# ScalarE takes the normalizing and the division of the router's weights in a fused four-layer kernel's last layer

## The reference

```python
x = x + _L3_xattn_ref(_layernorm(x, axis=-1), ctx_2048, itok_BxS_0_1023, ...)
x = x + _L3_ffn_ref(_layernorm(x, axis=-1), L3_ffn_gate_w, ...)

def _layernorm(x, axis=-1, eps=1e-05):
    m = jnp.mean(x, axis=axis, keepdims=True)
    v = jnp.var(x, axis=axis, keepdims=True)
    return (x - m) / jnp.sqrt(v + eps)

def _L3_ffn_ref(hidden_states, gate_w, gate_proj_w, up_proj_w, down_proj_w):
    x = hidden_states.reshape(-1, h)
    router_logits = x @ gate_w
    routing_weights, selected = jax.lax.top_k(router_logits, K)
    routing_weights = jax.nn.softmax(routing_weights, axis=-1)
    ...
    gate = jax.lax.ragged_dot(hidden_sorted, gate_proj_w, group_sizes)
    up = jax.lax.ragged_dot(hidden_sorted, up_proj_w, group_sizes)
    down = jax.lax.ragged_dot(jax.nn.silu(gate) * up, down_proj_w, group_sizes)
    ...
    out = jnp.sum(out * routing_weights[..., None], axis=1)
```

## Time and profile before

| | us |
|---|---|
| median of 3 runs | 755.91 |
| lowest and highest run | 755.21, 762.36 |
| profiled execution, its own time | 756.39 |
| its span on the core | 754.7 |
| mean granted TensorE clock | 0.953 of full |
| TensorE busy | 662.2 (88% of the span) |
| VectorE busy | 600.8 (80%) |
| ScalarE busy | 480.1 (64%) |
| GpSimd busy | 417.5 (55%) |

### The profile page before, as it was taken

The page is one execution under the profiler, slowest core; times in us unless marked ns, Lnnn a source line. Parts: engine busy times, 40 slices in busy tenths (PEclk is TensorE's granted clock), DMA queues, the critical chain, the costliest instruction groups (busy, mean ns, idle before and its releaser), DMA issues.

```text
span 754.7 us, 14577 instructions
## 1 busy us (share of the span) xinstructions
PE 662.2 (88%) x5052; PEld 552.6 (73%) x5052; DVE 600.8 (80%) x1657; ACT 480.1 (64%) x1203; POOL 417.5 (55%) x535
## 2 busy tenths in 40 slices
PE   2998969885799989969998988988888999999974
PEld 1887857663479845748887877877667999999942
DVE  6567368988956878888788998998788899999666
ACT  3543557956845378747776666666434699999810
POOL 2444683994610226414555377578774277777764
PEclk9999996989989999999999999999999899999998
DMA  8987003400010050039100011014336399999393
GB/s 326 311 263 249 8 2 83 145 1 1 3 44 1 1 210 2 1 110 369 41 1 1 1 48 56 33 49 175 106 134 218 116 318 320 314 322 314 121 374 141
DMA packets 47522, 100.63 MB, mean 133 GB/s; under 512 B 7349, under 2 KB 27782, under 8 KB 45940
## 3 DMA queue, kind: packets, MB, share of 16 engines
q1 hardware_dynamic: 40196, 82.46, 32.2%
q0 software_dynamic: 7248, 17.18, 6.2%
HBM read 60.17 MB, written 43.12 MB: 137 GB/s over the span
## 4 chain that ended last, share of the span: by engine, by line
PE 40%; DVE 34%; ACT 12%; POOL 6%; issue 5%; DMA 3%; SPq 0%; DVEq 0%; POOLq 0%; ACTq 0%
PE bank L320 9%; PE bank L321 8%; PE bank L322 8%; DVE sc L2036 3%; DVE qf L2050 3%; PE bank L2637 3%; DVE qf L2045 2%; ACT p L1988 2%; DVE X L2452 2%; DVE st L346 2%; ACT p L973 2%; DVE HN L366 1%; POOL hl L781 1%; DVE op6l L2025 1%; DVE qs L2044 1%
## 5 line engine op out<-in xcount | busy, mean ns | idle before, releaser
L2848 POOL DMA_INDIRECT rows_out<-ye,di x87 | 95.8, 1101 | 42.6 <-ACT ye L2725 21.5
L2085 POOL TENSOR_SCALAR p<-p,ri 128x256 f32<-128x256 f32 x128 | 74.0, 589 | 75.9 <-DVE ri L2030 75.1
L1988 ACT ACTIVATE p<-sc,mn 128x256 f32<-128x256 f32 x128 | 64.1, 502 | 37.3 <-DVE mn L2036 37.2
L2315 POOL DMA_INDIRECT slots_in<-row,si x64 | 67.2, 1050 | 16.6 <-issue 15.3
L320 PE MATMUL bank<-x7h,w7h 128*96 128x192 f32 x232 | 63.7, 275 | 0.0
L321 PE MATMUL bank<-x7l,w7h 128*96 128x192 f32 x232 | 59.4, 256 | 0.0
L322 PE MATMUL bank<-x7h,w7l 128*96 128x192 f32 x232 | 59.2, 255 | 0.0
L360 POOL TENSOR_TENSOR rs<-ve,neghalf 128x2 f32<-128x2 f32 x32 | 23.2, 728 | 58.4 <-DVE ve L354 58.0
L320 PE MATMUL bank<-w7h,h7h 96*128 96x256 f32 x164 | 49.2, 300 | 5.8 <-DVE h7l L2428 4.9
L1925 PE MATMUL bank<-ident,p 128*128 128x128 f32 x256 | 41.1, 284 | 14.1 <-POOL p L2085 13.5
L2142 DVE TENSOR_TENSOR w7l<-w7f,w7h 128x640 fp32r<-128x640 f32 x60 | 48.9, 815 | 2.4 <-ACT w7h L2137 2.1
(11 more groups left out here) (448 smaller groups left out, 2579.0 us busy)
## 6 DMA issues: line engine op xcount, KB each, us to landing
w7f<-in_w SPq DMA_DIRECT2D x64, 320.0 KB, 4.4
xe<-slots_in SPq DMA_DIRECT2D x29, 432.0 KB, 5.3
slots_in<-zt SPq DMA_DIRECT2D x7, 1728.0 KB, 19.1
rows_out<-zt SPq DMA_DIRECT2D x8, 1024.0 KB, 10.2
rw<-rows_out SPq DMA_DIRECT2D x4, 2048.0 KB, 9.5
w0raw<-in_w SPq DMA_DIRECT2D x3, 768.0 KB, 10.8
wo<-in_w_o SPq DMA_DIRECT2D x1, 2048.0 KB
raw<-in_w SPq DMA_DIRECT2D x2, 704.0 KB, 4.9
```

Of the source, the lines that this page charges most:

```text
L1988: a = A.activation(m.p6[k2 % 5][:, s, :], m.sc6[k2 % 3][:, s, :], ACT.Exp, bias=m.mn6[k2 % 5][:, s:s + 1], scale=-1.0, accum_out=m.su6[k2 ...
L2085: i = G.tensor_scalar(m.p6[j][:, s, :], m.p6[j][:, s, :], m.ri6[j][:, s:s + 1], 1.0, ALU.mult, ALU.mult)
L2315: G.indirect_dma_start(out=m.buf_in, out_offset=bass.IndirectOffsetOnAxis(ap=m.si7[:, t, j:j + 1], axis=0), in_=m.row7[:, t, :], in_offset ...
L2848: G.indirect_dma_start(out=m.buf_out, out_offset=bass.IndirectOffsetOnAxis(ap=m.di7[:, q:q + 1], axis=0), in_=m.ye7[q % NY][:], in_offset= ...
```

## The change

For pairs 0 to 2 in the attention stage the normalizing goes from VectorE to ScalarE. ScalarE computes it as `x * rs + sh`, so GpSimd makes the shift `sh = -mean * rs` first (`gpsimd_shift`, two instructions of one column, one for each tile, at ago 1 right behind the power). Pair 3's normalizing in `head` stays on VectorE. For all four pairs the division of all experts' weights by their sum (two instructions of 128x64) goes from VectorE to ScalarE, at ago 15 in `l3x` and after `h7h` of i = 3 in `head`; VectorE keeps the product of exponentials and mask.

```diff
-    def gpsimd_apply(self, g):
-
+    def gpsimd_shift(self, g):
         G, m = self.nc.gpsimd, self.m
         for t in (2 * g, 2 * g + 1):
             G.wait_ge(*self.rstd.at(g + 1))
             G.tensor_scalar(m.sh[:, t:t + 1], m.mv[:, t, 0:1], m.rs[:, t:t + 1], -1.0, ALU.mult,
                             ALU.mult).then_inc(self.shift.sem, 1)
+
+    def scalar_apply(self, g):
+        A, m = self.nc.scalar, self.m
+        for t in (2 * g, 2 * g + 1):
+            A.wait_ge(*self.shift.at(t + 1))
+            A.activation(self.rows[:, t, :], m.X[:, t, :], ACT.Identity, bias=m.sh[:, t:t + 1],
+                         scale=m.rs[:, t:t + 1]).then_inc(self.hn.sem, 1)
...
@@ l3x, scalar()
                 g, ago = routing(k)
+                if ago == 2:
+                    r.norm.scalar_apply(g)
...
+                if ago == 15:
+                    r.scalar_weights(g)
@@ l3x, vector()
-                if ago == 2:
-                    r.norm.vector_apply(g)
@@ l3x, gpsimd()
                 if ago == 1:
                     r.norm.gpsimd_rstd(g)
+                    r.norm.gpsimd_shift(g)
@@ Router
         V.tensor_tensor(m.wt7[:, p, :], m.ex7[:, 2 * (g % 2):2 * (g % 2) + 2, :],
                         m.mk7[:, 128 * g:128 * g + 128].rearrange("p (m n) -> p m n", m=2),
-                        ALU.mult).then_inc(self.wt.sem, 1)
-        V.wait_ge(*self.wt.at(3 * g + 1))
-        V.wait_ge(*self.rw.at(12 * g + 11))
+                        ALU.mult).then_inc(self.chosen.sem, 1)
+
+    def scalar_weights(self, g):
+        A, m = self.nc.scalar, self.m
+        A.wait_ge(*self.chosen.at(g + 1))
+        A.wait_ge(*self.rw.at(12 * g + 11))
         for t in (2 * g, 2 * g + 1):
-            V.tensor_scalar(m.wt7[:, t, :], m.wt7[:, t, :], m.r7[:, t:t + 1], None, ALU.mult).then_inc(self.wt.sem, 1)
+            A.activation(m.wt7[:, t, :], m.wt7[:, t, :], ACT.Copy, scale=m.r7[:, t:t + 1]).then_inc(self.wt.sem, 1)
@@ head, scalar()
             dense.scalar_high(i, i)
+            if i == 3:
+                r.scalar_weights(3)
@@ head, vector()
             if i == FIRST + 1:
-                V.wait_ge(*r.wt.at(12))
+                V.wait_ge(*r.wt.at(8))
```

More of the change, by code:

```diff
@@ L375, in gpsimd_apply @@
                             ALU.mult).then_inc(self.shift.sem, 1)
+    def scalar_apply(self, g):
[4 more added lines that the diff above has]
+                         scale=m.rs[:, t:t + 1]).then_inc(self.hn.sem, 1)
+    def gpsimd_apply(self, g):
+        G, m = self.nc.gpsimd, self.m
+        self.gpsimd_shift(g)
         for t in (2 * g, 2 * g + 1):
@@ L1849, in l3x @@
     done = m.xfinal = lambda t: x.at(t + 1)
-    m.next_norm = Norm(nc, m, sig, rows=m.row7[:, :, 0:D])
+    m.next_norm = Norm(nc, m, sig, rows=m.row7[:, :, 0:D], shifted=6)
     r, w7 = m.router, m.weights = Router(nc, io, m, sig), Weights(nc, io, m, sig)
@@ L2166, in __init__ @@
         m.scattered = sig("scattered", 16 * 64)
-        self.ng, self.ex, self.wt = sig("neg_top", 4), sig("exps_router", 8), sig("router_weights", 12)
+        self.ng, self.ex, self.wt = sig("neg_top", 4), sig("exps_router", 8), sig("router_weights", 8)
+        self.chosen = sig("exps_chosen", 4)
         self.rw = sig("row_weights", 48)
```

## The result

The changed kernel takes 761.15 us (759.17 to 766.98), the kernel before 757.12 (755.21 to 762.36), 12 runs of each on the same chip: ratio 1.0067, 95% interval [1.0045, 1.0089]. It is slower, by 4.0 us between the medians (by the interval 3.4 to 6.7), and outside the predicted range. Repeated on two more occasions it gave 1.005 [1.0023, 1.0077] and 1.007 [1.0035, 1.0104]. The profiled execution took 759.63 us (span 757.9), 3.2 us more than before.

What follows compares the result with a forecast made beforehand. It took the chain of hand-overs (GpSimd ahead of TensorE, VectorE from the logits on), not VectorE's busy share, as the bound; +0.81 + 0.14 - 0.42 = +0.53 us on 755.91 gave 756.4, 8-in-10 range 752.0 to 760.0.

Steps and rivals of the forecast that it cites:

- Part 1: Normalizing leaves VectorE, pairs 0 to 2: it starts at most 0.3 us earlier, then waits for TensorE's scores; gain 0.
- the 91% share: VectorE's busy share, 120.4 of 133 us in the 400 to 533 us window; argued for winning its time in full.
- Part 2: The two `sh` join GpSimd's queue ahead of scatter and `p` scalings: +0.81 us, all in front of TensorE.
- 0.13 + 0.34 + 0.34: Net GpSimd delay at pairs 0, 1, 2: 0.60 us for `sh` less 0.47, 0.26 and 0.26 coming back.
- the upper bound: If the `sh` fall beside `Ql` and are stretched by 0.47, they cost 1.4 us more: 2.2 us.
- the reason given for the scatter: At pairs 1 and 2 VectorE's normalizing, once gone, no longer stretches GpSimd's scatter: 1.31 back to 1.05 us, 0.26 each.
- all of it: The whole +0.81 us of GpSimd's delay over pairs 0 to 2 falls in front of TensorE.
- the pause of TensorE costs its clock once more: Rival: longer pause brings pair 2 the low clock, 1.43 us more, 757.8; chance 0.18 shared with a late ScalarE.
- a late ScalarE: Rival: slow normalizing or late shift delays `pt` and exponentials, three times up to 1.0 us, 759.4; shared chance 0.18.
- Part 4: Weights' scaling moves to ScalarE: +0.07 us each at pairs 0 and 1, 0 at pair 2, -0.42 at pair 3.
- VectorE loses 0.42 us on its chain ... So `Qh` comes 0.42 earlier: Weights, pairs 0 and 1: `Qh` 0.42 us earlier, what follows 0.49 later on ScalarE, +0.07 per pair.
- Part 3: ScalarE's two normalizing instructions between `op6h` and next `pt`: about 1.0 us, nine tenths covered by idle; cost 0.

Runs made afterwards that it cites:

- e4: Changed kernel with GpSimd's shift one step later, behind the next `p` scalings, and ScalarE's normalizing one step later: 804.03 us, ratio 1.0025 to the kernel before.
- e13: Changed kernel with 16 (pair 0) and 24 (pairs 1, 2) extra TensorE products in the pause ahead of the `p` transposes: 757.59 us, ratio 0.9999.
- e14: Kernel before with 12 and 16 extra TensorE products in the pause ahead of the `p` transposes: 756.01 us, ratio 0.9979.
- e3: Kernel before with the six shift instructions added on GpSimd behind the power, read by nobody; normalizing stays on VectorE: 804.24 us, ratio 1.0048.
- e2: Kernel before with only the weights' scaling moved to ScalarE, for all four pairs: 805.89 us, ratio 1.0049.
- e5: Kernel before with the weights' scaling on ScalarE, placed ahead of `Qh` in the same step: 758.54 us, ratio 1.002.
- e1: Changed kernel with the weights scaled on VectorE again, so only the normalizing half: 802.97 us, ratio 0.999.
- e6: Kernel before with GpSimd's power one step later, behind the `p` scalings, and VectorE's normalizing one step later: 757.34 us, ratio 1.0008.
- e9: Changed kernel with power and `sh` behind `p`, ScalarE's normalizing a step later and the weights, both ahead of `Qh`: 801.9 us, ratio 1.0024; again 753.67, 0.9954.
- e7: Changed kernel with power and `sh` one step later, behind the `p` scalings, and ScalarE's normalizing one step later, behind `Qh`: 757.07 us, ratio 0.9993.
- e10: As e9, but ScalarE normalizes right behind that step's `pt`, ahead of the exponentials: 801.7 us, ratio 1.0055.
- e11: Kernel before with power behind `p`, weights on ScalarE ahead of `Qh`, VectorE normalizing between the minima and `qs`: 808.53 us, ratio 1.0088.

## Why the prediction was wrong

The forecast was +0.5 us, to 756.4, with a range of 752.0 to 760.0. Measured were 761.15 against 757.12, and for the profiled executions 759.63 against 756.39.

**Part 1, VectorE gains nothing: right.** It waits 0.81 us for `op6h` where it normalized, and longer for the scores. The chain of waits beat the 91% share.

**Part 2, +0.81 us in front of TensorE: too small, and its agreement with the outcome is luck.** The first `p` transpose starts 0.43, 0.67 and 0.66 us later behind the variance than before (2.83, 4.19 and 4.18 against 2.39, 3.52 and 3.52), together 1.76, more than twice the 0.13 + 0.34 + 0.34. The term that was mis-sized is `sh`: it costs the queue 0.9 us a pair and not 0.6, because it was stretched, which I had put at the upper bound (0.80 us for the pair where I wrote 0.50). What comes back from `p` and the scatter was about as forecast (0.47 and 0.21), though the reason given for the scatter was wrong (e4). At the logits only half of the delay is left. With the clock held full in both kernels (e13 against e14) the three stretches cost -0.05, +0.49 and +0.45, together +0.89. At pair 0 a later wait of TensorE takes it up; the changed kernel's clock held (e13) and the kernel before's (e14):

```profile
413.42 0.36 PE L1908 MATMUL bank<-qch,QW6h 96*128 96x256 f32 x1 [0.62 <-ACT hT L2229]
```

```profile
414.19 0.36 PE L1897 MATMUL bank<-qch,QW6h 96*128 96x256 f32 x1 [1.12 <-ACT hT L2214]
```

So 0.89 is close to 0.81 because two errors cancel, the second being that "all of it" would reach the end of the stretch.

The stretch beside `Ql` is what the Trainium skill, "GPSIMD Engine Reference", section Specifications, describes as contention on the shared SBUF interfaces with VectorE instructions of two SBUF inputs. The trace agrees (0.80 us beside `Ql`, 0.49 and 0.50 without), and for instructions of one column as well, which I had excused for their size.

**The step that failed: the sum carries TensorE's clock at nothing.** It appears only as a rival, "the pause of TensorE costs its clock once more", at a chance of 0.18 shared with a late ScalarE and a price of 1.43 us, once. It is what happened, and larger. The sum of the low clock rose from 6.8 to 17.0 us over the three stretches. By after minus e13 it costs 4.85 us, by before minus e14 1.13: +3.7 us from this alone. By the medians the filled pauses give back 4.5 us in the changed kernel and 1.7 in the one before, 2.8 more, with 2 to 3 us of uncertainty on each. What makes a low stretch last 6.8 us and not 3.4 behind the longer pauses is open (e3 has the pauses without it); that the clock is what costs the time, and that filled pauses take it away, is shown. I had the mechanism and the pair where it would strike, but four things wrong. The pauses grew by 1.1 us, not by 0.3: besides the 0.66 of the queue there are 0.47 us by which the variance falls further behind TensorE once the weights stand on ScalarE's chain (e2). The low stretch could also double in length (pair 1: 3.4 to 6.8). I made it wait for a pause of "about 2.6", with 2.3 not enough, though in the kernel before the clock had fallen behind pauses of 1.85 and 2.32. And I took pair 2's full clock in the one trace as a coin that could fall either way, with the gains set against the losses, where the repeats show nearly the same pattern every time (e5, whose attention stage is timed like before's, 3.4, 3.4, 0 as well; the changed kernel 6.8 at pair 2 in three of three).

**Part 4, weights: +0.14 forecast, +0.92 measured** for pairs 0 and 1, between their logits and the next variances. The failed step is "VectorE loses 0.42 us on its chain ... So `Qh` comes 0.42 earlier". Right behind the scalings stood `op6l`, and its `op6h` ends 0.4 us after the product does (445.43 in the rows above): the same wait that I had counted at the other end of the step, but not here. The rest of the step was exact (0.49 on ScalarE; the wait 0.76 where I wrote 0.7 to 0.8). Placed ahead of `Qh`, the same work costs nothing (e5). For pair 2, 0 forecast, -0.11 measured. **For pair 3, -0.42 forecast, -0.41 measured.**

**Part 3, ScalarE's normalizing: right in what it says of the queue,** 1.09 us against 1.0, with the following exponential's idle gone; e3, without it, has pauses as long as e1. That it has no part in the longer low clock is not shown, for e3 lacks that too.

The sum by what was measured: 0.9 (queue) + 3.7 (clock) + 0.9 (weights) - 0.1 - 0.4 = +5.0 us, the difference of the cut stretches.

## What to carry to other kernels

Before adding to an engine's queue, look at what it delays on TensorE, and price the clock with the wait: here 0.9 us of queue and 0.9 of late weights came with 3.7 us lost to the half clock, and up to 24 products to no purpose in each pause took those away. Freed time is only won if the instruction next in line is ready; follow the freed engine to its very next wait before subtracting anything. And a small step costs by its place, not by its engine: the 0.49 us of the weights were free in ScalarE's idle time ahead of its wait for `qf`, and paid in full behind it.

## What the runs showed of the hardware

- The low clock is not a function of the pause alone. It was low for 3.4 us behind a pause of 2.32 and not at all behind 2.31 in the same execution, and not behind 3.07 (e3, pair 1). Full clock throughout the stage was seen in the kernels whose pauses were filled or split (e6, e9, e13, e14), though e7, e10 and e11 each lost it once or twice with the pause at `p` gone.
- GpSimd's instructions of 128x1 go from 0.50 us a pair to 0.80 (0.88 with VectorE's normalizing following, e3) beside one `Ql`, and a scatter from 1.05 to 1.29 to 1.32.
- A ScalarE activation of 128x256 with a per-lane scale and bias takes 0.59 to 0.60 us (two of them 1.09 from start to end), the exponential with a per-lane bias alone 0.49 to 0.51.
